# First layer: GpSimd sums the exponential blocks of every chunk, and the Newton steps of the output rows run three groups later

## The reference

```python
h = jnp.maximum(_layernorm(x, axis=-1), 0.0)
q = (h @ Wq.T + bq)   # and k, v; 4 heads of 64
scores = jnp.einsum('bhnd,bhjcd->bhnjc', q, kc) / sqrt(Dh)   # 8 chunks of 256 keys
scores = jnp.clip(scores, -10.0, 10.0)
scores = jnp.where(mask == 0, -10.0, scores)
attn = jax.nn.softmax(scores, axis=-1)                # within each chunk of 256 keys
ctx = jnp.einsum('bhnjc,bhjcd->bhnd', attn, vc)       # summed over the chunks
out = ctx @ Wo.T + bo + h                             # the block's residual is its own input
out = (out - mu) * rsqrt(var + EPS) * gamma + beta
x = x + out
```

## Time and profile before

| what | value |
|---|---|
| time, median of 3 runs | 4523.58 us (4523.34 to 4524.16) |
| the profiled execution, its own time | 4522.35 us |
| its span in the trace | 4520.6 us |
| busy: PE, DVE, ACT, POOL | 96%, 76%, 66%, 69% of the span |
| layer 0 | from the start to about 2857 us, the rest is layer 1 |
| period of one batch in layer 0 | 350.1 us |

### The profile page before, as it was taken

The page is one execution under the profiler, slowest core; times in us unless marked ns, Lnnn a source line. Parts: engine busy times, 40 slices in busy tenths (PEclk is TensorE's granted clock), DMA queues, the critical chain, the costliest instruction groups (busy, mean ns, idle before and its releaser), DMA issues. The chain is left out here.

```text
span 4520.6 us, 83340 instructions
## 1 busy us (share of the span) xinstructions
PE 4328.3 (96%) x34312; PEld 2531.1 (56%) x34312; DVE 3414.3 (76%) x4242; ACT 2977.7 (66%) x3498; POOL 3109.9 (69%) x2262
## 2 busy tenths in 40 slices
PE   7999999999999999999999999399999999999997
PEld 3334334334334334333333333299999999999997
DVE  4875875776776776776687677388888988889885
ACT  3664664664665665566566466188888888878885
POOL 4685685675675676676577477367787868778785
PEclk9999999999999999999999999699999999999999
DMA  6001001001001000000000000111120212212111
GB/s 200 10 10 38 10 10 30 19 10 29 20 10 29 20 10 28 20 8 27 15 10 20 10 10 20 54 34 55 48 83 27 76 33 71 67 38 81 32 57 43
DMA packets 126973, 160.82 MB, mean 36 GB/s; under 512 B 8833, under 2 KB 109185, under 8 KB 126593
## 3 DMA queue, kind: packets, MB, share of 16 engines
q1 hardware_dynamic: 126592, 155.49, 11.0%
HBM read 121.64 MB, written 33.83 MB: 34 GB/s over the span
## 5 line engine op out<-in xcount | busy, mean ns | idle before, releaser
L585 ACT ACTIVATE e_sb<-e_sb 128x1024 f32<-128x1024 f32 x1024 | 1081.2, 1057 | 898.2 <-DVE e_sb L687 861.2
L687 DVE SCALAR_TENSOR_TENSOR e_sb<-psS,mask 128x1024 f32<-128x1024 f32 x1024 | 1202.7, 1216 | 436.5 <-PE psS L816 435.9
L1426 PE MATMUL psA<-xy,ring_p 128*128 128x195 bf16 x8192 | 1398.1, 248 | 9.7 <-DVE red L1303 9.7
L1426 PE MATMUL psA<-xy,ring_s 128*128 128x195 bf16 x8192 | 1397.8, 248 | 0.0
L418 POOL TENSOR_TENSOR e_sum<-e_sb 128x1024 f32<-128x1024 f32 x384 | 918.5, 2392 | 463.1 <-ACT e_sb L585 331.5
L1222 ACT ACTIVATE ring_s<-eiB,ejb 128x1024 int8<-128x1024 f32 x1024 | 1088.5, 1135 | 9.9 <-PE psA L1426 9.9
L816 PE MATMUL psS<-qT,kT 64*128 64x512 f32 x4096 | 1020.0, 616 | 4.6 <-DVE e_sb L687 4.5
L829 PE MATMUL psN<-e_sb,v_sb 128*32 128x512 f32 x8192 | 985.2, 598 | 12.5 <-ACT num L523 12.5
L1426 PEld LDWEIGHTS psA<-xy,ring_p 128*128 128x128 fp8e4 x8192 | 799.3, 98 | 13.7 <-DVE red L1303 11.5
L1426 PEld LDWEIGHTS psA<-xy,ring_s 128*128 128x128 fp8e4 x8192 | 798.4, 97 | 7.9
L816 PEld LDWEIGHTS psS<-qT,kT 64*128 64x128 f32 x4096 | 351.7, 186 | 642.4 <-issue 404.8
(11 more groups left out here) (117 smaller groups left out, 4246.9 us busy)
## 6 DMA issues: line engine op xcount, KB each, us to landing
eiB<-ei_between SPq DMA_DIRECT2D x64, 512.0 KB, 4.3
xin<-x SPq DMA_DIRECT2D x32, 512.0 KB, 3.8
xr<-x SPq DMA_DIRECT2D x32, 512.0 KB, 4.8
x_between<-hy SPq DMA_DIRECT2D x32, 512.0 KB, 3.2
xin<-x_between SPq DMA_DIRECT2D x32, 512.0 KB, 5.6
xo<-x_between SPq DMA_DIRECT2D x32, 512.0 KB, 4.3
out<-o_sb SPq DMA_DIRECT2D x32, 512.0 KB, 5.2
xr<-adjT SPq DMA_DIRECT2D x24, 512.0 KB, 4.2
```

Source lines behind the costliest of these rows:

```text
L585: act.activation(e_sb[:, n % ES], e_sb[:, n % ES], ACT.Exp, scale=SCALE).then_inc(exp_done, 1)
L687: dve.scalar_tensor_tensor(out=e_sb[:, n % ES], in0=psS[:, s % 2], scalar=-CLIP_RAW, in1=mask[:, kb, cols][:, None, :].to_broadcast([P, 2, ...
L1426: ins = pe.matmul(psA[:, i % BANKS, br * PARTS * XW:(br + 1) * PARTS * XW], part[:, n % RING, k, tt * TW + j * P:tt * TW + (j + 1) * P], x ...
```

## The change

SUMMED becomes GPH = 8: POOL adds the two blocks of all eight groups of a half, so the branch with eight products (L842) is never taken again and all chunks go through the four products on `e_sum`. The last chunk's denominators move from the even iteration to the odd one behind it, and now wait for POOL. The `stop` flag of the products follows. The Newton steps of the output rows move from iterations 15, 15, 16, 17 after a tile's end to 18, 18, 19, 20, and ACT's scaling that needs them from 19, 21 to 22, 24.

```diff
-OUT_AT, STAT2_AT, AGGR2_AT, RSQRT2_AT = 11, 12, 14, (15, 15, 16, 17)
-YN_AT, AFFINE_AT = (19, 21), 28
+OUT_AT, STAT2_AT, AGGR2_AT, RSQRT2_AT = 11, 12, 14, (18, 18, 19, 20)
+YN_AT, AFFINE_AT = (22, 24), 28
...
-        SUMMED = GPH - PAIRS
+        SUMMED = GPH
...
                     for hd in range(H):
                         ins = pe.matmul(psD[32 * hd:32 * hd + 32, :], hot[:, c, :], e_sum[:, (q + hd // 2) % SUMS, hd % 2, :],
-                                        start=c == 0, stop=False, skip_group_check=True)
+                                        start=c == 0, stop=c == CPH - 1, skip_group_check=True)
```

## The result

| | before | changed |
|---|---|---|
| median of the runs | 4523.66 us (20 runs; 19 of them 4521.32 to 4527.56) | 4530.64 us (20 runs, 4528.39 to 4533.19) |
| ratio, 95% interval | | 1.0015 (1.0009 to 1.0022) |
| profiled execution: own time, span | 4522.35, 4520.6 us | 4531.79, 4530.0 us |

What follows compares the result with a forecast made beforehand. PE was taken as gapless from group to group, but POOL's late sums and ACT's wait were to leave 2.7 us of the 55 removed: 4519.7 us profiled, 4520.9 us as median (1.2 above), range 4506 to 4535.

Steps and rivals of the forecast that it cites:

- PE's gain: In each of 64 halves, four products replace eight on PE, saving 0.86 us each, 55 us in all.
- The walk through POOL's queue: POOL's operations timed one by one against PE's need: sums late by 0.26 and 0.69 us in the third tile.
- The fourth tile, -2.85: Tile with the next batch's Newton steps: 1.72 + 0.08 gained, 2.78 lost to late sums, 1.87 to ACT: 2.85 us lost.
- both idle times: PE in the fourth tile: 2.52 us for the sum of group 55; wait for ACT's copy growing from 1.55 to 3.4.
- the preparation: Last half's denominators there: 0.56 us gained, since some 0.3 of 0.86 goes to the projection waiting for DVE's copy `hT`.
- The end of layer 0: Two more sums ahead of POOL's last four context additions cost 4.65 us once; its end moves by under 4 us.
- The three signs: Forecast wrong if PE waits nowhere for POOL, L707's median leaves 0.745 us, or POOL's sums start later than every 2.33.
- the first falls: Rival: POOL keeps up and PE gives all 55 us, 4469 us; chance 0.05.
- the second falls: Rival: ACT's wait for the Newton steps costs nothing (13 us better, 4508) or the two small latenesses vanish; chance 0.2.
- The third: Rival: slower, POOL's big operations start every 2.39 us instead of 2.33 in the packed stretch, 14 us, 4535; chance 0.22.
- the port: DVE and POOL contend for SBUF; fuller POOL might mean more long L707: 8 to 9 us, 4529, 1 in 10.
- the main case: POOL's lateness eats most of PE's gain, L707 still slips between small POOL operations; 4512 to 4530 us, chance 0.53.

Runs made afterwards that it cites:

- the last kernels: Changed kernel with next batch's Newton steps in iterations 27 to 30 and sums before context additions: 4473.08 us; `turn_h` later too: 4466.88; last-batch `b_o`, `be_row` later too: 4465.11.
- the kernel with the filled gaps: Changed kernel, but PE issues its score products twice in iterations 57 and 59 of batches 0 to 6, values unchanged: 4523.49 us.
- the sums alone: Changed kernel with all eight sums per half, but the output rows' Newton steps and ACT's scaling in their old iterations: 4548.38 us.
- the move alone: Kernel before the change with only the output rows' Newton steps and ACT's scaling three iterations later, no added sums: 4524.32 us.
- the sums ahead of the additions: Changed kernel, but in each iteration POOL makes the sum before the context addition: 4521.54 us.
- the early Newton steps: Changed kernel with the next batch's Newton steps in iterations 27 to 30 in place of 54 to 57: 4498.75 us.

## Why the prediction was right, and where it failed

The forecast was a gain of 2.7 us and the measurement a loss of 7. That 4530.64 lies inside the range is luck: its upper end was priced for a slower POOL, which did not happen.

- **PE's gain** (0.86 us for four products) was right: the first tile gives -0.86, and the last kernels give nearly all of the 55 us.
- **The walk through POOL's queue** held. Third tile -0.78 against -0.85, second -1.00 against -1.02 (batch 0: -1.72, as forecast), sum of group 55 late by 2.42 against 2.52, and PE's wait for ACT 3.49 against 3.4. ACT's wait for `nmr` is 1.83 in batches 1, 3 and 5, where 1.9 was forecast; in batches 0, 2, 4 and 6 the scores come later by the low clock, and 0.42 is left of it.
- **The fourth tile, -2.85, is the step that failed.** Without the clock it is -3.1, as the kernel with the filled gaps shows in seven batches. In the changed kernel 2.7 us more are lost in batches 1, 3 and 5, 8.1 us in all, since PE's granted clock falls behind the idle times. The prediction had both idle times with their sizes and priced them as time in which nothing happens; it did not ask what PE's clock does behind them, so the clock is a term that stands at nothing in its sum, and in none of its rivals. Taking 8.1 from the 9.4 us by which the profiled execution grew leaves +1.3, where the sum said -2.7: without the clock the kernel would have come out level, still not faster. The 7 us between the medians of the changed kernel and the filled one agree.
- **What is left of the miss** is 4.0 us: the fourth tile 7 x 0.2 = 1.4, the preparation 7 x 0.19 = 1.3 (-0.37 in place of -0.56), the third tile 8 x 0.07 = 0.6, the projection at the end 0.45 (the clock once more) and layer 1 0.5, less 0.4 by which the first group starts earlier, to within 0.2. In the preparation the forecast 0.3 before the projection is there (it starts 2.04 after the numerators, which take 1.74 from start to start), but the four products do not stand ahead of it: they split it in two, and the two halves take 3.60 + 3.53 us from start to start where the whole took 6.97 (721.35 to 728.32).

```profile
719.77 1.92 PE L827 MATMUL psN<-e_sb,v_sb 128*32 128x512 f32 x16
721.81 3.67 PE L759 MATMUL psS<-hT,w_s 128*128 128x512 f32 x8
725.41 1.07 PE L846 MATMUL psD<-e_sum,hot 128*32 128x512 f32 x8
726.41 3.70 PE L759 MATMUL psS<-hT,w_s 128*128 128x512 f32 x8
729.94 1.89 PE L759 MATMUL psS<-w_s,hT 128*128 128x256 f32 x8
```

- **The end of layer 0**: 4.65, as forecast, for the additions. It was to lie under 4 us from where it was and lies 8.9 later (2852.11 against 2843.18). The three signs that were to show the forecast wrong did not come: PE does wait for POOL, L705's median is 744 ns, and POOL's pace is unchanged. None of them looked at the clock.
- **Rivals.** PE does wait for POOL, so the first falls. ACT's wait does cost, so the second falls. The third named the right sign by the wrong cause: big operations still start every 2.31 to 2.33 (676.33 to 678.66, 682.16 to 684.47 in POOL's timeline). As to the port: a fuller POOL did not mean more long L705. Least, median and most are as before (741, 744 and 2877 ns against 741, 745 and 2883), but only 8 of 64 are over a microsecond, where 24 were before. It is the move of the Newton steps that does this, not the sums: 25 with the sums alone, 9 with the move alone. So L705 did slip in between the small operations, as the main case had it, and PE waits for it 10.6 us in all, 11.3 before. The rows of POOL in batch 1:

```profile
676.33 2.38 POOL L433 TENSOR_TENSOR ctxT<-ctxT,num 128x1024 f32<-128x1024 f32 x1
678.66 2.35 POOL L416 TENSOR_TENSOR e_sum<-e_sb 128x1024 f32<-128x1024 f32 x1
...
682.16 2.35 POOL L433 TENSOR_TENSOR ctxT<-ctxT,num 128x1024 f32<-128x1024 f32 x1
684.47 2.38 POOL L416 TENSOR_TENSOR e_sum<-e_sb 128x1024 f32<-128x1024 f32 x1
```

and the line L705 on DVE (count, then least, median and greatest duration in ns, then the first and last start in us):

```profile
L705 DVE SCALAR_TENSOR_TENSOR r_s<-r_s,lo_rows,r_f x64: 741/744/2877, 124.9 to 2830.3; 128x512 fp32r<-128x512 f32 x64
```

## What to carry to other kernels

Work that goes from the bounding engine to one with idle time on average arrives as lateness at single places: walk the helper's queue operation by operation against the time at which each result is wanted, and move away whatever stands there without being urgent (here the place of a few small steps and the order within an iteration turned 7 us lost into 51 gained, and `turn_h` an iteration later into 57). An idle time of PE that a change makes or lengthens can have a second price, the clock of what comes behind it: look for it in a window view of a few microseconds, since a slice of the page is too coarse, and fill the gap where it can't be closed.

## What the hardware showed that I had not expected

In a kernel where PE is busy 95% of the span, the granted clock fell to 0.50 once in every batch that prepares a next one: behind idle times of 2.42 and 3.49 us, or already behind the first. With the sums alone it fell behind 0.78 and 3.49, with the sums ahead of the additions behind 0.44 and 5.80. With the early Newton steps (0.49 and 1.55 us idle) and in the kernel with filled gaps (0.70 and 1.77) it stayed at 1.00. Numerators took 3.64 us in place of 1.92 there, denominators 1.96 in place of 1.07. The Trainium skill ("TensorE: Matmul & The Clock Gate", Part 1: The HAM clock gate) says that a gate passes half or all of the pulses by how busy PE has lately been; the trace agrees, with 0.50 in the slow stretches and 1.00 around them. What the fall costs depends on where it lands: 2.7 us in front of work that all wait for, nothing that can be seen where PE has to wait again right behind. Which batch gets which goes by turns, and with the sums alone the turns are the other way round (batch 0 loses more, batch 1 less). What sets them stays open.
